# Second attention's loop: a group's application in three parts over three slots, its output moved to later slots

## The reference

```python
q = rope((x @ Wq).reshape(b, t, 32, 16).transpose(0, 2, 1, 3))
k = rope((x @ Wk).reshape(b, t, 8, 16).transpose(0, 2, 1, 3))
v = (x @ Wv).reshape(b, t, 8, 16).transpose(0, 2, 1, 3)
scores = einsum('bhqd,bhkd->bhqk', q, repeat(k, 4)) / sqrt(16)
attn = softmax(where(causal, lowest, scores))
ctx = einsum('bhqk,bhkd->bhqd', attn, repeat(v, 4)) @ Wo
```

## Time and profile before

| | |
|---|---|
| median of 3 runs | 1178.65 us (1178.55 to 1179.78) |
| the profiled execution's own time | 1180.05 us |
| its span, first to last instruction | 1178.4 us |
| the loop of the second attention | from 914.1 us to 1097.9 us of the span |
| busy share of the span: TensorE, VectorE, ScalarE, GpSimd | 97%, 66%, 60%, 35% |
| mean granted clock of TensorE | 0.996 of full |

### The profile page before, as it was taken

How to read it: one execution, slowest core, us unless ns; L and a number is a source line. 1 busy time by engine, 2 the same in 40 slices (tenths; PEclk the granted TensorE clock), 3 DMA queues, 4 the chain that set the end, 5 groups by cost and what they waited for, 6 DMA issues and landing times. The chain is left out here.

```text
span 1178.4 us, 20479 instructions
## 1 busy us (share of the span) xinstructions
PE 1138.7 (97%) x6634; PEld 954.3 (81%) x6634; DVE 778.3 (66%) x2463; ACT 705.6 (60%) x1646; POOL 410.9 (35%) x342
## 2 busy tenths in 40 slices
PE   7899999999999999999999999999999899999997
PEld 6788888888888888888888778888888677777786
DVE  6767776667776677766677762222336799999775
ACT  6666665566665566666566544543113799999524
POOL 4554554355444455534443513434013210010200
PEclk9999999999999999999999999999999999999999
DMA  6011110101110110100100012222001223321001
GB/s 230 19 36 37 40 33 28 31 28 36 47 36 20 38 31 24 55 27 11 45 19 28 1 37 80 62 80 73 1 18 28 50 71 78 100 52 34 2 1 72
DMA packets 30364, 51.24 MB, mean 43 GB/s; under 512 B 5680, under 2 KB 6576, under 8 KB 30256
## 3 DMA queue, kind: packets, MB, share of 16 engines
q1 hardware_dynamic: 29680, 48.85, 14.4%
q10 hardware_dynamic: 576, 1.05, 0.2%
HBM read 38.35 MB, written 2.10 MB: 34 GB/s over the span
## 5 line engine op out<-in xcount | busy, mean ns | idle before, releaser
L487 POOL TENSOR_TENSOR turned<-turned,sin 128x512 f32<-128x512 f32 x73 | 94.5, 1294 | 311.6 <-ACT turned L347 311.6
L363 ACT ACTIVATE probs<-probs,neg_max 128x256 f32<-128x256 f32 (+1 forms) x256 | 119.8, 473 | 14.0 <-DVE neg_max L580 14.0
L1477 ACT ACTIVATE a_probs<-a_probs,a_neg_max 128x512 f32<-128x512 f32 (+3 forms) x256 | 122.6, 563 | 0.1
L1661 DVE CUSTOM_DVE_ANT_0 a_probs<-bank,a_mask 128x512 f32<-128x512 f32 (+3 forms) x256 | 109.8, 486 | 7.8 <-PE bank L1881 7.8
L490 POOL TENSOR_TENSOR turned<-turned,by_cos 128x512 f32<-128x512 f32 x73 | 101.2, 1386 | 5.7
L96 PE MATMUL bank<-wo_hi,oT_hi 128*128 128x512 f32 x256 | 100.3, 392 | 1.6 <-DVE oT_lo L643 1.6
L734 PE MATMUL bank<-xT_hi,wq_hi 128*128 128x512 f32 x256 | 101.7, 397 | 0.0
L734 PE MATMUL bank<-xT_lo,wq_hi 128*128 128x512 f32 x256 | 100.3, 392 | 0.0
L734 PE MATMUL bank<-xT_hi,wq_lo 128*128 128x512 f32 x256 | 100.1, 391 | 0.0
L96 PE MATMUL bank<-wo_hi,oT_lo 128*128 128x512 f32 x256 | 99.9, 390 | 0.0
L96 PE MATMUL bank<-wo_lo,oT_hi 128*128 128x512 f32 x256 | 99.7, 389 | 0.0
(11 more groups left out here) (234 smaller groups left out, 3158.8 us busy)
## 6 DMA issues: line engine op xcount, KB each, us to landing
staged<-weights SPq DMA_DIRECT2D x70, 256.0 KB, 2.7
f_staged<-weights_f SPq DMA_DIRECT2D x33, 256.0 KB, 2.7
a_q_stack<-a_qT_hi SPq DMA_DIRECT2D x64, 64.0 KB, 2.0
rows<-x_rows SPq DMA_DIRECT2D x2, 1024.0 KB, 7.4
a_k_stack<-a_kT_hi SPq DMA_DIRECT2D x64, 32.0 KB, 2.0
a_q_stack<-a_qT_lo SPq DMA_DIRECT2D x32, 64.0 KB, 2.0
out<-rows SPq DMA_DIRECT2D x8, 256.0 KB, 2.0
a_raw<-weights_qkv SPq DMA_DIRECT2D x4, 384.0 KB, 4.4
```

What stands on the lines that cost most here:

```text
L363: act.activation(probs[:, s % 2, h, 0:width], probs[:, s % 2, h, 0:width], ACT.Exp, bias=neg_max[:, s % 2, h:h + 1], scale=SCALE0, accum_o ...
L487: pool.tensor_tensor(at, at, sin[:, :], ALU.mult).then_inc(sin_done, 1)
L1477: act.activation(row_probs(s, qt), row_probs(s, qt), ACT.Exp, bias=neg_max[:, h, qt:qt + 1], scale=-1.0).then_inc(exp_done, 1)
L1661: dve.tensor_tensor_reduce(row_probs(s, qt), ps_s[bank][:, at:at + seen], mask[:, SEQ - seen:SEQ], -SCALE1, HIGHEST, ALU.add, ALU.min, neg ...
```

## The change

The application of a group is cut in three parts instead of two: keys 0 in the group's slot class 0, keys 1 in class 1, keys 3 and 2 in class 2, the last of them ahead of `turn` (class is s % 4). The semaphore `applied` so counts three for each group. The copy of the output moves from class 2 to class 3; the transposes move from class 3 to class 0 of the next group, behind its first part; the join moves from class 3 to class 1 of the next group. The loops of TensorE and VectorE run one slot further, so that the last group is finished.

```diff
-APPLY_KEYS = ((0, 3), (1, 2))
+APPLY_KEYS = ((0,), (1,), (3, 2))
+APPLY_PARTS = len(APPLY_KEYS)
...
@@ ScalarE, copy_turned
-                    act.wait_ge(applied, 2 * ((s - RING) // GROUP1 + 1))
+                    act.wait_ge(applied, APPLY_PARTS * ((s - RING) // GROUP1 + 1))
@@ VectorE, copy_turned and evacuate
-                    dve.wait_ge(applied, 2 * ((s - RING) // GROUP1 + 1))
+                    dve.wait_ge(applied, APPLY_PARTS * ((s - RING) // GROUP1 + 1))
...
-                dve.wait_ge(applied, 2 * (n + 1))
+                dve.wait_ge(applied, APPLY_PARTS * (n + 1))
@@ VectorE, the loop
-            for s in range(SLOTS1 + 3):
-                if s % GROUP1 == 2 and s >= GROUP1:
+            for s in range(SLOTS1 + 4):
+                if s % GROUP1 == 3 and s >= GROUP1:
                     evacuate(s // GROUP1 - 1)
...
-                if s % GROUP1 == 3 and GROUP1 <= s < SLOTS1:
-                    join(s // GROUP1 - 1)
+                if s % GROUP1 == 1 and 2 * GROUP1 <= s < SLOTS1 + GROUP1:
+                    join(s // GROUP1 - 2)
@@ TensorE, the loop
-            for s in range(SLOTS1 + 2):
+            for s in range(SLOTS1 + 3):
+                if s >= GROUP1 and s % GROUP1 == 2:
+                    apply(s // GROUP1 - 1, 2)
                 if s < SLOTS1:
                     turn(s)
                 if s >= GROUP1 and s % GROUP1 < 2:
                     apply(s // GROUP1 - 1, s % GROUP1)
                 if s == 0:
                     scores(2)
-                if s % GROUP1 == 3 and s >= GROUP1:
-                    turn_output(s // GROUP1 - 1)
+                if s % GROUP1 == 0 and 2 * GROUP1 <= s < SLOTS1 + GROUP1:
+                    turn_output(s // GROUP1 - 2)
                 if s + AHEAD_SCORES < SLOTS1:
                     scores(s + AHEAD_SCORES)
```

## The result

The changed kernel takes 1184.91 us (median of 5 runs, 1184.67 to 1186.41), the kernel before 1178.58 us on the same chip (5 runs, 1178.47 to 1179.78). The ratio is 1.0053, with a 95% interval of 1.0042 to 1.0064: 6.3 us slower, outside the 0.2% that a measurement can't tell from no change. Forecast were 1185.6 us and +6.9.

What follows compares the result with a forecast made beforehand. Bound by hand-overs between TensorE and VectorE, no engine alone. Steady loop 6.0, head -0.1, tail 1.0: 6.9 us more, the profiled 1180.05 becoming 1187.0, the median 1.4 lower, 1185.6; range 1180.0 to 1190.0.

Steps and rivals of the forecast that it cites:

- The ring of today and the ring after: Hand-overs between TensorE and VectorE closing on one group's period in the second attention's loop: 11.04 us today, 11.50 after.
- T0 to S0: Class 0 on TensorE, from start of turn to start of scores: forecast 2.66 us, bounds 2.46 and 2.86.
- The change-overs: On TensorE, switching between kinds of matmul costs 0.11 us out of an application and 0.17 into it.
- 13 groups: Steady loop, slots 8 to 59: each group 0.46 us longer, 6.0 us in all.
- Head: Loop start: slot 4's application saves up to 0.4 us, given back in slots 6 and 7; together -0.1 us.
- Tail: Loop end: slot 60 0.23 us longer, slot 61 0.22, uncovered output transposes 0.45 + 0.11; together 1.0 us.
- Idle times: VectorE waits about 1.3 us for scores before class 1's maxima; TensorE about 0.9 before class 0's turn.
- C2 "just in time": VectorE's copy of turned probabilities in class 2 due 4.51 us after class 1's maxima, its transposes ready at 4.49.
- (a): Smoothing works, faster: TensorE's own 10.61 us per group becomes the period, total 1174.0 us; chance 0.09.
- (b): No change: output transposes hide behind class 0's application, period 11.04 to 11.14, total 1179.5 to 1181 us; chance 0.11.
- (c): Class 2's application ahead of turn delays VectorE's copy by 0.3, period 11.8, total 1189.5 us; chance 0.10.
- (d): TensorE's clock falls in every second group of the loop, 11 us more, total 1197 us; chance 0.04.

Runs made afterwards that it cites:

- kernel before again: The kernel before, unchanged, profiled once more in two draws: 1178.16 and 1178.26 us; the clock was 1.00 in 930 to 933 in its second profile.
- changed kernel again: The changed kernel, unchanged, profiled once more: 1184.57 us, clock 1.00 in 930 to 933.

## Why the prediction was right

By its own steps, against the pair of profiles without the drop of the clock (kernel before again, changed kernel again):

- **The ring of today and the ring after.** Right in place and order. Its terms: T0 to S0 2.66 forecast, 2.62 measured; S0 to M1 0.65 and 0.62; M1 to M2 2.87 and 2.88; M2 to M3 2.84 and 2.84; M3 to T0 2.48 and 2.47. Sum 11.50 and 11.43. Of the two misses the larger, 0.04, lies in the one stretch that the trace of before did not show, output transposes between an application and the scores: they took 0.41, not 0.45. The other is S0 to M1 behind them, 0.03.
- **The change-overs.** The change-over behind an application was there as taken, not free: A0 to O is 1.00 (1022.53 to 1023.53) for passes of 0.89. By the rule that the prediction cites, and that its rows contradict, the time would have been 1184.2, by the rows 1185.6; 1184.91 lies between and does not decide, the rows do. The prediction also put that rule without its condition: the Trainium skill, "TensorE: Matmul & The Clock Gate", Part 2, has weight loads pulled ahead where the row groups do not conflict or the load goes to the background buffer. Behind the scores of the changed kernel a load is pulled ahead by 0.10 us, behind an application none is (last section).
- **13 groups.** 6.0 forecast. From slot 8 to slot 60 the kernel before took 1084.33 - 940.90 = 143.43, the changed one 1089.55 - 940.94 = 148.61: 5.2. This is the largest term that was off, by the 0.07 per group above.
- **Head.** -0.1 forecast, slot 8 starts at 940.90 and 940.94: nothing. The 0.4 that the forecast let slot 4 save belonged to the lower clock, which neither of these two profiles had; it was not tested.
- **Tail.** 1.0 forecast. From slot 60 to the first output transposes after the loop it was 1095.97 - 1084.33 = 11.64 and is 1102.31 - 1089.55 = 12.76: 1.1. Its parts were less even: 0.17 in slot 60 and 0.72 for the transposes behind the last group's first part, where 0.23 and 0.56 were forecast.
- **What follows the loop** shifts as a whole: 6.3 at the loop's end, 6.4 in the span.
- **Idle times.** Before M1 1.3 forecast, 1.15 recorded. Class 3 lasts 2.70 for 1.77 of work, 0.93 lost where 0.9 was forecast; but only 0.31 of it stands before T0. The rest is lost inside the scores of class 3, whose second piece waits for the maxima (1031.06 and 1031.71 in the rows above). The forecast's sign, some 0.9 idle before T0, was wrong in that; that the copy ends the wait was right.
- **C2 "just in time"** held in the changed kernel: no idle time there. It became a bound in the variant with only the order on TensorE changed.

Of the rivals, (a) falls with the place of keys 3: moving work between slots changes the time though TensorE's sum stays. It was not empty, though: with the scores first the smoothing works, at 10.35, below the 10.61 that I had for TensorE alone, since two applications then run into each other (the row of 24 passes), one change between kinds less in each direction. (b) falls, the transposes do not hide behind an application. (c) did not come about: the application ahead of T2 is not in the ring of the changed kernel. (d) did not either: the clock is 1.00 in the steady loop of every kernel here. That loop has scores in every slot and applications beside the transposes, so it does not show whether transposes alone would hold the clock.

One figure of the forecast does not follow from its terms: its own range ends at 1188.4, its bounds at 1188.2.

Right by luck in part: the base of the sum. The first profile of the kernel before held the drop of the clock, and the 1.4 by which I put the median below it is that drop. For the profiled execution the forecast was 1187.0, and it took 1184.90, since it did not meet the drop. To judge by the times, one of five executions met it on either side (1179.78 and 1186.41); with unequal shares the measured difference could have moved by 1.5 either way, and the forecast had no term for that.

## What to carry to other kernels

Where several engines exchange single buffers and each is over 90% busy, the sum of one engine's work is only a lower bound; write down the start-to-start distances of one period and follow the ring of hand-overs that closes on the period exactly. Moving work evens an engine's slots but pays only if it leaves the ring, and a piece put between an instruction that was waited for and the one that the other engine waits for costs its full length. So the order within a slot comes first: release the other engine (here the scores), then do what nobody waits for (here the application), and put VectorE's extra copy where it would wait anyway. Together these places were worth 9 us against the kernel before (16 against the changed one); the number of parts, in a like order, was worth nothing.

## What the hardware showed that I had not expected

TensorE's clock fell at the loop's head in some executions and not in others of the same program. In the first profile of the kernel before it was 0.60 over 930 to 933, after a stretch in which TensorE was busy 1.78 of 3.00 us; in the second it was 1.00 there, after a stretch with 1.64 of 3.00 busy. The variant with the output copy ahead of C2 had the same 1.64 and fell, to 0.53. So the busy share just before does not tell the two apart, and what does is open. In single microseconds the first profile shows 0.81 from 930 to 931 and 0.50 in each of the three that follow: the mean of 0.60 is part of the time at 2.4 and most of it at 1.2 GHz. The cost is read between the two profiles from slot 4 to slot 8: 942.82 - 930.16 = 12.66 us against 940.90 - 929.87 = 11.03, 1.6 us. In the steady loop, ten transposes in every slot, the clock stayed at 1.00 in all thirteen profiles, also in the changed kernel with its idle time of 0.9 in class 3.

Behind an application in 32-column tiles the next weight load did not start early, in any kernel's steady loop. In the changed kernel the load for the output transposes stands 0.99 us behind the start of an application (1022.53) whose passes take 0.89 by size, while the load for T1 starts 0.10 ahead of T1 (1024.66), with the scores still running:

```profile
1023.52 0.42 PEld L1933 LDWEIGHTS bank<-identity,a_oT_now 128*128 128x128 f32 x4 [0.84 <-issue]
...
1024.56 1.12 PEld L1900 LDWEIGHTS bank<-identity,a_probs 128*128 128x128 f32 x10
```

Why the load waits in one case and not in the other is not shown.
